# A two-phase language-model block: constants prepared on GpSimd, bias rows stored earlier, last expert added in SBUF and written plainly

## The reference

```python
h = _L0_tok_ref(x, ...)                       # embedding, attention, softmax over axis 1
h = h + _L0_attn_ref(_layernorm(h), ...)      # in_proj, conv, SSD scan, y * silu(z), RMS norm * norm_w, out_proj
h = h + _L0_ffn_ref(_layernorm(h), ...)
# in _L0_ffn_ref:
slot = jnp.where(valid, bin_ids * capacity + offsets, E * capacity)
xb = jnp.zeros((E * capacity + 1, hs), x.dtype).at[slot].set(xf[src])
h = jax.nn.gelu(jnp.einsum('ech,ehf->ecf', xb, w1))
y = jnp.einsum('ecf,efh->ech', h, w2).reshape(E * capacity, hs)
out = jnp.zeros((T, hs), x.dtype).at[src].add(flat_w[order][:, None] * yv)
return out.reshape(sl, bs, hs) + bias
```

## Time and profile before

| | |
|---|---|
| median of 3 runs | 974.99 us (973.57 to 975.16) |
| the profiled execution | 972.38 us |
| its span, first to last instruction | 970.6 us |
| PE busy | 893.6 us (92%) |
| DVE busy | 634.4 us (65%) |
| ACT busy | 529.2 us (55%) |
| POOL busy | 493.9 us (51%) |
| chain of work that ended last | PE 80%, DVE 10%, issue 3%, DMA 2%, POOL 2% |

### The profile page before, as it was taken

One profiled execution on the slowest core, in us unless ns is written; L12 is line 12 of the kernel. 1 busy time (PEld: TensorE's weight loads), 2 busy tenths in 40 slices (PEclk: granted clock), 3 DMA queues, 4 the chain that ended last, 5 costly groups with the idle time before them and its releaser, 6 DMA issues.

```text
span 970.6 us, 17232 instructions
## 1 busy us (share of the span) xinstructions
PE 893.6 (92%) x5580; PEld 790.1 (81%) x5580; DVE 634.4 (65%) x1665; ACT 529.2 (55%) x1094; POOL 493.9 (51%) x491
## 2 busy tenths in 40 slices
PE   5699999999999999999998629999999999999992
PEld 4588888888888888888886419999999999999992
DVE  3477898888988898888986333636463636363620
ACT  1467777677677767677665123545444544444330
POOL 2157776887678777887677221232333232323322
PEclk9899999999999999999997659999999999999996
DMA  7920111001000000000000034344343433342121
GB/s 228 325 63 6 39 38 40 22 33 32 12 22 17 19 13 24 22 13 23 12 22 13 13 100 137 70 106 94 81 107 71 108 71 103 71 108 29 21 24 22
DMA packets 49038, 57.58 MB, mean 59 GB/s; under 512 B 6208, under 2 KB 44715, under 8 KB 49008
## 3 DMA queue, kind: packets, MB, share of 16 engines
q1 hardware_dynamic: 34992, 41.23, 13.3%
q0 software_dynamic: 14016, 15.97, 10.7%
HBM read 33.09 MB, written 29.75 MB: 65 GB/s over the span
## 4 chain that ended last, share of the span: by engine, by line
PE 80%; DVE 10%; issue 3%; DMA 2%; POOL 2%; SPq 1%; ACT 1%; DVEq 0%; POOLq 0%
PE bank L1536 12%; PE bank L1538 12%; PE bank L1537 12%; PE bank L1334 11%; PE bank L1443 5%; PE bank L1279 4%; PE bank L1424 4%; PE bank L1318 3%; PE bank L1300 3%; PE bank L1309 3%; PE bank L1293 2%; PE bank L1396 2%; DVE seg L1019 2%; PE bank L1458 2%; PE bank L1548 2%
## 5 line engine op out<-in xcount | busy, mean ns | idle before, releaser
L627 POOL DMA_INDIRECT out<-ye,tok_slot x64 | 110.7, 1730 | 286.0 <-DMA out<-ye,tok_slot 155.2
L837 ACT ACTIVATE hf<-bank 128x512 f32<-128x512 f32 x128 | 79.3, 619 | 203.6 <-PE bank L1538 203.6
L1232 DVE TENSOR_TENSOR h_lo<-hf,h_hi 128x512 fp32r<-128x512 f32 x128 | 88.7, 693 | 104.7 <-ACT h_hi L839 104.7
L1536 PE MATMUL bank<-w_hi,h_hi 128*128 128x256 f32 x512 | 146.1, 285 | 0.0
L1537 PE MATMUL bank<-w_lo,h_hi 128*128 128x256 f32 x512 | 144.9, 283 | 0.0
L1538 PE MATMUL bank<-w_hi,h_lo 128*128 128x256 f32 x512 | 144.9, 283 | 0.0
L991 DVE SCALAR_TENSOR_TENSOR xc<-bank,cw,xc 128x253 f32<-128x253 f32 (+2 forms) x288 | 128.2, 470 | 1.7
L1536 PE MATMUL bank<-xe_hi,w_hi 128*128 128x512 f32 x256 | 100.9, 394 | 2.7 <-DVE xe_lo L1224 2.7
L1537 PE MATMUL bank<-xe_lo,w_hi 128*128 128x512 f32 x256 | 100.5, 393 | 0.0
L1538 PE MATMUL bank<-xe_hi,w_lo 128*128 128x512 f32 x256 | 100.4, 392 | 0.0
L578 POOL DMA_INDIRECT slots_dram<-rows,slot x64 | 63.4, 990 | 71.8 <-DVE slot L1120 57.2
(11 more groups left out here) (200 smaller groups left out, 2289.7 us busy)
## 6 DMA issues: line engine op xcount, KB each, us to landing
w_raw<-w SPq DMA_DIRECT2D x16, 1024.0 KB, 8.3
slots_dram<-zero_row SPq DMA_DIRECT2D x1, 8320.0 KB, 29.9
xe<-slots_dram SPq DMA_DIRECT2D x16, 520.0 KB, 4.7
out<-hb SPq DMA_DIRECT2D x16, 256.0 KB, 2.1
w_raw<-in_wT SPq DMA_DIRECT2D x1, 1288.0 KB, 8.9
slots_dram<-rows,slot POOLq DMA_INDIRECT x64, 2.2
out<-ye,tok_slot POOLq DMA_INDIRECT x64, 3.8
xg<-emb,idx POOLq DMA_INDIRECT x36, 3.9
```

Source lines behind the costliest of these rows:

```text
L627: g.indirect_dma_start(out, bass.IndirectOffsetOnAxis(ap=tok_slot[q][:, j:j + 1], axis=0), ye[q][:, j, :], None, compute_op=ALU.add).then_ ...
L837: sc.activation(hf[m % 2][:, :], h_bank[i % H_BANKS][:, :], ACT.Gelu_apprx_tanh)\
L1232: vc.tensor_tensor(h_lo[:, m, :], hf[m % 2][:, :], h_hi[:, m, :].bitcast(F32), ALU.subtract)\
L1536: te.matmul(out_, hi, rhi, start=first_, stop=False)
```

## The change

There are three parts.

**Start.** The ten small loads are issued by ACT with a semaphore of their own (`s_small`); SP issues only the seven large ones, and `w_in` (`s_win`), `w_out` (`s_wout`) and the query and key weights (`s_qk`) have their own semaphores. PE's `wqk` waits for the two weights alone. The fill of the slot memory waits for `w_in` and `w_out`. The split of `w_in` and the scaling of `w_out` leave DVE and stand on POOL behind its gathers; PE's `project_out` waits in each half for `w_out_ready`.

**Border.** In the two halves of the drain without a front part, `with_bias` stands first in POOL's half instead of behind `free_rows`. POOL waits for the last stores before it gives `part_done`.

**Last expert.** POOL first fetches the current output rows of the expert's 1024 tokens into SBUF (`fetch_sums`, eight indirect loads into `base`). DVE weighs and adds in one instruction per 128 rows (`weigh_onto`), and POOL writes the sums with indirect DMAs without an add (`write_sums`), still one after the other. For the last group PE gives each of the four row blocks a bank of its own (`last_product`) and signals each, so that DVE and POOL take them one by one.

```diff
-            for dst, src in early:
-                sp.dma_start(dst, src).then_inc(s_early, 16)
-            for dst, src in loads:
-                sp.dma_start(dst, src).then_inc(s_consts, 16)
+            sp.dma_start(wqk_in[:, 0, :, :], w_qT.rearrange("(k p) n -> p k n", p=P)).then_inc(s_qk, 16)
+            sp.dma_start(wqk_in[:, 1, :, :], w_kT.rearrange("(k p) n -> p k n", p=P)).then_inc(s_qk, 16)
+            sp.dma_start(posT[:, :, :], pos_encT).then_inc(s_early, 16)
+            sp.dma_start(wv[:, :, :], w_v.rearrange("(k p) n -> p k n", p=P)).then_inc(s_early, 16)
+            sp.dma_start(w_in[:, :, :], in_wT.rearrange("(k p) n -> p k n", p=P)).then_inc(s_win, 16)
+            sp.dma_start(w_out[:, :, :], out_wT.rearrange("(k p) n -> p k n", p=P)).then_inc(s_wout, 16)
 
             sp.wait_ge(s_template, 1)
-            sp.wait_ge(s_consts, 16 * N_LOADS)
+            sp.wait_ge(s_win, 16)
+            sp.wait_ge(s_wout, 16)
...
@@ block.gpsimd
-            pool.wait_ge(s_consts, 16 * N_LOADS)
+            pool.wait_ge(s_small, 16 * N_SMALL)
+
+            pool.wait_ge(s_win, 16)
+            g.tensor_copy(w_dt[:, :, :], w_in[:, :, DI + CC:])
+            g.tensor_copy(w_in_hi[:, :, :], w_in).then_inc(w_in_split, 1)
+            pool.wait_ge(w_in_split, 1)
+            g.tensor_tensor(w_in_lo[:, :, :], w_in, w_in_hi[:, :, :].bitcast(F32), ALU.subtract)\
+                .then_inc(w_in_split, 1)
+            pool.wait_ge(s_wout, 16)
+            g.tensor_tensor(w_out[:, :, :], w_out[:, :, :], bc(nw[:, :].unsqueeze(2), [P, KI, DM]), ALU.mult)\
+                .then_inc(w_out_ready, 1)
...
             def half(p, f, b, t, nf):
                 q = 1 - p
+                if t and not f:
+                    with_bias(t, p)
                 if b:
                     decayed_x(b, q)
...
                     free_rows(t, p)
+                if t and f:
                     with_bias(t, p)
...
                 pool.wait_ge(scattered[p], 64 * PAIRS)
-            pool.wait_ge(hb_ready.sem, 2 * PAIRS)
+                pool.wait_ge(hb_stored[p], hb_stored.credit * (PAIRS + 1))
             pool.sem_inc(part_done, 1)
...
+            def fetch_sums():
+
+                for j in range(JS):
+                    g.indirect_dma_start(base[:, j, :], None, out,
+                                         bass.IndirectOffsetOnAxis(ap=tok_slot[1][:, j:j + 1], axis=0))\
+                        .then_inc(fetched, 16)
+
+            def write_sums():
+
+                for j in range(JS):
+                    hold(pool, ye_ready, 2 + (NE - 1) * (JS // 2) + (j // 2 + 1 if j < JS // 2 else j + 1 - JS // 4))
+                    g.indirect_dma_start(out, bass.IndirectOffsetOnAxis(ap=tok_slot[1][:, j:j + 1], axis=0),
+                                         ye[1][:, j, :], None).then_inc(added, 16)
+                    pool.wait_ge(added, 16 * (JS * (NE - 1) + j + 1))
+                pool.sem_inc(expert_added, 1)
+
             def experts(r, last):
-                for q in range(2):
-                    add_results(r * 2 + (q - 1), q)
+                add_results(r * 2 - 1, 0)
+                if last:
+                    pool.wait_ge(slot_info, NE)
+                    fetch_sums()
+                    write_sums()
+                else:
+                    add_results(r * 2, 1)
@@ block.scalar
+            for dst, src in small:
+                act.dma_start(dst, src).then_inc(s_small, 16)
             act.wait_ge(s_wqk, 1)
             sc.activation(wqk[:, :, :].rearrange("p k n -> p (k n)"), bank[0][0][:, :], ACT.Copy,
                           scale=float(DM) ** -0.5).then_inc(s_wqk, 1)
-            act.wait_ge(s_consts, 16 * N_LOADS)
+            act.wait_ge(s_small, 16 * N_SMALL)
@@ block.vector
+            dve.wait_ge(s_masks, 1)
+            vc.tensor_copy(below_r[:, :], below[:, :]).then_inc(s_below, 1)
...
-            dve.wait_ge(s_consts, 16 * N_LOADS)
-            dve.wait_ge(s_masks, 1)
-            prep.mark(vc.tensor_copy(below_r[:, :], below[:, :]))
-            prep.wait()
-            vc.tensor_copy(w_dt[:, :, :], w_in[:, :, DI + CC:])
-            vc.tensor_copy(w_in_hi[:, :, :], w_in).then_inc(w_in_split, 1)
-            dve.wait_ge(w_in_split, 1)
-            for k in range(KI):
-                vc.tensor_scalar(w_out[:, k, :], w_out[:, k, :], nw[:, k:k + 1], None, ALU.mult)
-            vc.tensor_tensor(w_in_lo[:, :, :], w_in, w_in_hi[:, :, :].bitcast(F32), ALU.subtract)\
-                .then_inc(w_in_split, 1)
+            dve.wait_ge(s_small, 16 * N_SMALL)
...
+                def weigh_onto(g):
+
+                    half = g % NG
+                    if half == 0:
+                        dve.wait_ge(fetched, 16 * JS)
+                    for j in range(4 * half, 4 * half + 4):
+                        if half == 0:
+                            row, at = y_bank[j // 2], (j % 2) * DM
+                            dve.wait_ge(y_psum, Y0 + 4 * NG * (NE // 2 - 1) + 2 * g + j // 2 + 1)
+                        else:
+                            row, at = LAST_BANKS[j - 4], 0
+                            dve.wait_ge(y_psum, Y0 + 4 * NG * (NE // 2 - 1) + 2 * g + j - 4 + 1)
+                        ins = vc.scalar_tensor_tensor(out=ye[1][:, j, :], in0=row[:, at:at + DM],
+                                                      scalar=w_slot[1][:, j:j + 1], in1=base[:, j, :],
+                                                      op0=ALU.mult, op1=ALU.add)
+                        if half or j % 2:
+                            ins.then_inc(ye_ready, 1)
...
-                    weigh(g)
+                    if last and g >= NG:
+                        weigh_onto(g)
+                    else:
+                        weigh(g)
@@ block.tensor
-            pe.wait_ge(s_early, 16 * N_EARLY)
+            pe.wait_ge(s_qk, 32)
...
                 def project_out(r, p):
+                    pe.wait_ge(w_out_ready, 1)
...
+                def last_product(g):
+
+                    for j in range(4):
+                        if j < 2:
+                            pe.wait_ge(ye_ready, r * (4 * NG) + (2 * g + j + 1 - 4 * NG))
+                        for m in range(KF):
+                            if j == 0:
+                                pe.wait_ge(hlo_ready, r * PER_TURN + (2 + KF * g + m + 1 - PER_TURN))
+                            at = slice(m * DM, (m + 1) * DM)
+                            ins = three(LAST_BANKS[j][:, 0:DM], h_hi[:, m, j * P:(j + 1) * P],
+                                        h_lo[:, m, j * P:(j + 1) * P], w_hi[1][:, 1, at], w_lo[1][:, 1, at],
+                                        m == 0, m == KF - 1)
+                        ins.then_inc(y_psum, 1)
```

41 lines of the change are left out of this document (23 added, 18 removed).

## The result

The changed kernel took 958.35 us (median of 4 runs, 957.14 to 958.6), the kernel before beside it 974.28 (4 runs, 972.34 to 975.16): ratio 0.9837 with an interval of 0.9818 to 0.9855, so 15.9 us faster. The prediction had the sign, but 9.5 us and a range that ends at 962.5: its size was wrong. The profiled execution of the changed kernel took 958.16 us with a span of 956.4; against the profile shown before (972.38) that is 14.2 us. The other 1.7 lie in which execution was profiled.

The account below looks back on a forecast made before the run. PE was 80% of the path, so gains could come only where PE is not fed: start 0.3, border 3.5, drain -0.2, end 5.9, in sum 9.5 us off 974.99, giving 965.5 us; 8-in-10 range 962.5 to 971.5.

Parts of the forecast that it names:

- Start: Start of the kernel: 0.8 us gained at `nmax` less 0.5 for small loads, 0.3 us gained, between +0.8 and -4.4.
- `nmax` can start at 22.8: At the start, `nmax` follows the scores once DVE's preparation goes to POOL, 22.8 in place of 23.59: 0.8 us gained.
- The 0.5 us set aside for the ten small loads: At the start, small loads running beside the gathers cost 0.5 us, with bounds of nothing and 5.2 us.
- POOL's new work: At the start, preparing constants on POOL takes 7 to 11.8 us, hidden before POOL is needed at 30.02; costed at nothing.
- I cost it at 0.2 us lost: Second-last half: `hb` now ahead of `xdec` moves it 1.3 us later, hidden by 0.3; 0.2 us lost, bounds 0 and 1.3.
- The fourth rival: Whole kernel: PE gives the shift back in waits and clock phases, time within 0.2% of 975; chance 0.06.
- Border: Border of the phases: the slots' load starts at 566.9 in place of 570.37, behind the last scatter; 3.5 us gained.
- End: Last expert: POOL's chain of eight plain writes lands at 961.0 in place of 966.9; 5.9 us gained.
- 3.7 that "stays": After the last landing: the remaining 3.7 us of the span are the program's close and do not change.
- about 5 us after PE's last product: Sign at the end: the last write is issued about 5 us after PE's last product is out.
- The second rival: Last expert: plain writes land as slowly as adds, 6.9 us lost in place of 5.9 gained, 978.3 us; chance 0.07.
- the first rival: Last expert: fetches land late or issue slowly, the end gains only 1.3 us, 970.1 us in all; chance 0.13.

Follow-up runs that it names:

- e15: Kernel before, with dummy products on PE in the gaps of the first half alone: 972.14 us, ratio 0.9985.
- e9: Kernel before, with 1.4 us of dummy products on PE once ahead of the second half: 974.17 us, ratio 1.0009.
- e16: Kernel before, with only the preparation of the constants moved from DVE to POOL, loads and first product as before: 965.76 us, ratio 0.9921.
- e3: Kernel before plus the end part alone (fetches, plain writes, with the border's wait for the last stores): 971.26 us, ratio 0.9978.
- e5: Kernel before, with dummy products on PE in the gaps of the drain and at the border: 966.72 us, ratio 0.9955.
- e6: Changed kernel, with dummy products on PE in the gaps of the drain and at the border: 961.80 us, ratio 0.9889.
- e14: Changed kernel, with 0.9 us of dummy products on PE once ahead of the second half: 959.58 us, ratio 0.9859.
- e1: Kernel before plus the start part alone (loads, preparation on POOL, first product): 966.08 us, ratio 0.9927.
- e13: Kernel before plus the start part alone, but PE's first product waits for all four early weights again: 965.95 us, ratio 0.9921.
- e10: Changed kernel, with 1.9 us of dummy products on PE once ahead of the second half: 965.15 us, ratio 0.9913.
- e8: Changed kernel, with the eight fetches waited for in halves by two semaphores instead of all at once: 955.42 us, ratio 0.9829.

## Why the prediction was wrong, step by step

- **Start, wrong: 0.3 against 3.8 us up to the third-last half.** The step that failed reads "`nmax` can start at 22.8: 0.8 us gained, and what is late next is the PE chain itself". It took the PE chain's durations as fixed. The runs showed the scores at 1.99 or 3.78 us, by the level, and with DVE free the short ones count (`nmax` at 20.77 in place of 22.8); before, they could not (e15, e9). Up to the third-last half the move is worth some 2 us with scores of 3.78 us and another 2 with scores of 1.99. Of the first 2, at most the 0.73 us of e16 is the move's direct gain at `nmax`, and none of it is left where the small loads land as early as in e3 and e5; the rest is open. That the changed kernel's profile has scores of 1.99 us is luck in part: e6, the same kernel up to the drain, and e14 had 3.78. The 0.5 us set aside for the ten small loads was not seen: the transposes started at 12.15, not later than 12.47.
- **POOL's new work, right.** 2.32 + 5.63 + 1.89 us, hidden, from 14.52 to 24.4: 9.9 us, in the bounds of 7 to 11.8. The upper bound laid the 1.85 ns per element of the earlier trace rows on the subtraction and on the conversion, 4.8 us each; the subtraction took 5.63, the conversion 2.32. DVE does the same subtraction in 2.83 us and the conversion in 1.50 (e15), so POOL is slower at both, and the move is the best part of the change all the same: here POOL's longer time was hidden, and DVE's could stand on the path.
- **Drain, wrong: -0.2 against +3.5 us.** The step that failed is the term "I cost it at 0.2 us lost", the only one for this stretch: it priced the moved instructions and put the level at nothing. `hb` ahead of `xdec` was hidden as said. The gain is no moved instruction: e1, e13 and e16 move none there and drain in 30.95 to 31.26 us, with 1.9 us of dummy products the changed kernel has the old drain of 34.6 (e10), and filled, the kernel before has one of 29.55 (e5). What the runs showed in its place is the level, down for 10 us in place of 24. How an edit at the start brings that about in most executions stays open. The fourth rival named clock phases, as a way to give the gain back, and had no price for them; the price, 3.5 us, and the sign were what was missing.
- **Border, right.** 3.5 predicted, 3.4 measured.
- **End, right in mechanism, too large: 5.9 against 2.7 us.** The first write was 1.0 us sooner than worked out (925.62 + 11.5 = 937.1, for 938.1), since the last fetch landed in 2.7 us, not 3.9. The seven steps took 23.65 us in place of 20.7: a landing of 2.4, not 2.2, and 0.76 to the next start make 3.2, and two of the steps took 3.7 and 3.8. After the last landing (951.7) the span runs 4.7 us on, in place of the 3.7 that "stays". And 2.7 is one pair of profiles: in all of them the stretch from the last add of expert seven to the end takes 50.6 to 52.3 us without this part, 48.7 to 50.7 with it and a single wait for the fetches, 2.2 us less on average, near the 2.1 of e3's times. PE's last product was out 0.8 us later than before, measured from that add, not 3.2; the sign "about 5 us after PE's last product" does not follow from the prediction's own sum (958.8 - 956.2 = 2.6), and 7 were measured. The second rival (writes as slow as adds) is out: 2.4 against 3.5 to 4.1 for the last eight adds of the kernel before, to the same rows.
- **Fetches as the wait, the first rival: no.** They were in at 923.85, which is 935.4 in the prediction's count, for its 936.4. But the wait for all eight was worth 3.6 us, which the prediction did not ask for (e8).

The range was too narrow because all its bounds were bounds of transfers and waits. None allowed for the level, though the profile of before showed it: the eight matmuls of 3.78 and of 1.99 us at the start, and the page's row of clocks, in tenths of full speed, with 8 in the second slice and 7, 6 and 5 at the drain and the border.

```profile
PEclk9899999999999999999997659999999999999996
```

## What to carry to other kernels

Where PE is fed with gaps, its durations in one profile can be those of one of two levels, as the 3.78 and the 1.99 us of the scores here: price a shifted stretch at both before calling it hidden, and repeat the profile. Work taken off an engine that runs beside such a stretch can count for more than its visible overlap: here 2.8 us at `nmax` in place of 0.8, in an execution in which the stretch ran at the higher level. Of a serial chain of transfers, ask first what starts it: here the wait for all eight fetches ahead of the first write was worth 3.6 us (e8).

## What the runs showed of the hardware

- 0.9 us more of dummy products cost the changed kernel 5.6 us by the medians, in addition to the 1.2 of the first 0.9; in the profiles TensorE's level then stayed at 0.50 for 24 us in the drain and not for 10 (e10, e14). One code has its scores at 1.99 us in the changed kernel's profile and at 3.78 in e6's. With edits at the start alone (e1, e13, e16) the level was down for 10 us in the drain 500 us later and the drain took 30.95 to 31.26 us, in place of 24 and 34.60; with 1.4 us of dummy products alone (e9) it was down for 24 us, and the drain took 34.51. How the start sets it is open.
- Products that compute nothing made a kernel 5.5 us faster (e5) and another one 3.4 slower (e6).
- A plain indirect write of 128 rows to rows of the output landed in 2.4 us, the last eight adds of the kernel before to the same rows in 3.5 to 4.1, the last fetch in 2.7. In e8 and in the changed kernel the wait ahead of the fourth write was 0.3 us longer than those around it (2.58 against 2.27).
- DVE's `neg_a`, 128x8, took 2.28 us beside POOL's conversion and 0.16 where POOL was idle (e15). The 2.28 us is longer than the 1.35 of `lm` beside `hb`, and cost nothing here.
